# Layer 3's queries: stored as whole fp32 words by one eviction each, split into high and low part on GpSimd at load

## The reference, cut to what matters

```python
B, Q, S1, S2 = (4, 64, 512, 512)
D, H, K, F = (512, 16, 128, 2048)
def _cross_attention(q_in, kv_in, wq, bq, wk, bk, wv, bv, wo, bo, bias_k, bias_v):
    qh = (q_in @ wq + bq).reshape(b, q_len, H, K)
    kh = (kv_in @ wk + bk).reshape(b, t, H, K)
    vh = (kv_in @ wv + bv).reshape(b, t, H, K)
    kh = jnp.concatenate([kh, jnp.broadcast_to(bias_k, (b, 1, H, K))], axis=1)
    vh = jnp.concatenate([vh, jnp.broadcast_to(bias_v, (b, 1, H, K))], axis=1)
    logits = jnp.einsum('bqhk,bthk->bhqt', qh, kh) / scale
    weights = jax.nn.softmax(logits, axis=-1)
    ctx = jnp.einsum('bhqt,bthk->bqhk', weights, vh).reshape(b, q_len, H * K)
    return ctx @ wo + bo
```

## Time and profile before

| what | value |
|---|---|
| time, median of 3 runs | 2662.59 us |
| lowest and highest run | 2662.57 and 2664.82 us |
| span of the profiled execution | 2669.9 us |
| own run time of the profiled execution | not given |
| PE (matmul) busy | 2463.5 us, 92% |
| PEld (weight load) busy | 2167.2 us, 81% |
| DVE busy | 1386.4 us, 52% |
| ACT busy | 1151.4 us, 43% |
| POOL busy | 752.3 us, 28% |
| mean granted TensorE clock | 0.954 |
| DMA | 459.14 MB, mean 172 GB/s |

### The profile page before, as it was taken

The page is one execution under the profiler, slowest core; times in us unless marked ns, Lnnn a source line. Parts: engine busy times, 40 slices in busy tenths (PEclk is TensorE's granted clock), DMA queues, the critical chain, the costliest instruction groups (busy, mean ns, idle before and its releaser), DMA issues. The chain is left out here.

```text
span 2669.9 us, 37770 instructions
## 1 busy us (share of the span) xinstructions
PE 2463.5 (92%) x13976; PEld 2167.2 (81%) x13976; DVE 1386.4 (52%) x2360; ACT 1151.4 (43%) x2473; POOL 752.3 (28%) x386
## 2 busy tenths in 40 slices
PE   7898689989999699899899999979998999999698
PEld 5676334479896467799899999979998999999698
DVE  4666631268886633233366565633335656664632
ACT  3777112123332432223476666622236666664320
POOL 1100322262210450341153342406204343432300
PEclk9999879989999799899999999999999999999799
DMA  7553163489995146344876666525287666663300
GB/s 232 128 134 70 69 226 112 110 245 231 246 235 177 67 176 230 130 151 155 285 242 216 211 201 188 190 82 192 105 289 259 196 195 215 220 203 110 118 12 25
DMA packets 237306, 459.14 MB, mean 172 GB/s; under 512 B 90588, under 2 KB 133620, under 8 KB 236356
## 3 DMA queue, kind: packets, MB, share of 16 engines
q1 hardware_dynamic: 237124, 456.73, 55.1%
HBM read 345.46 MB, written 119.37 MB: 174 GB/s over the span
## 5 line engine op out<-in xcount | busy, mean ns | idle before, releaser
L2007 PE MATMUL att_ring<-ca_pp,att_arena 128*128 128x400 f32 (+1 forms) x2304 | 429.1, 344 | 9.6 <-issue 7.1
L2007 PEld LDWEIGHTS att_ring<-ca_pp,att_arena 128*128 128x128 f32 (+1 forms) x2304 | 415.4, 188 | 15.9 <-issue 15.9
L2077 POOL TENSOR_TENSOR att_arena<-att_arena 128x1448 fp32r<-128x1448 f32 x64 | 212.4, 3319 | 611.1 <-ACT att_arena L2084 611.1
L2007 PE MATMUL att_ring<-att_arena,qk_wh 128*128 128x362 f32 x1024 | 256.3, 332 | 0.0
L2699 DVE TENSOR_TENSOR ca_yl<-att_ring,att_arena 128x400 fp32r<-128x400 f32 x256 | 146.5, 572 | 188.4 <-ACT att_arena L2657 188.4
L2007 PE MATMUL att_ring<-att_arena,qk_wl 128*128 128x362 f32 x512 | 173.2, 338 | 18.4 <-POOL att_arena L2264 17.2
L2007 PEld LDWEIGHTS att_ring<-att_arena,qk_wh 128*128 128x128 f32 x1024 | 185.6, 192 | 0.0
L2657 ACT ACTIVATE att_arena<-att_ring 128x400 fp32r<-128x400 f32 x256 | 129.0, 504 | 82.7 <-PE att_ring L2007 82.7
L2090 ACT ACTIVATE att_kstage<-att_score,att_shift 100x362 f32<-100x362 f32 x256 | 143.9, 563 | 45.4 <-DVE att_shift L2103 45.3
L1075 ACT ACTIVATE rec_stage<-rec_fbank,rec_columns 128x361 f32<-128x361 f32 x128 | 72.2, 564 | 199.0 <-PE rec_fbank L2007 198.3
L2007 PE MATMUL att_score<-att_arena 128*100 128x362 f32 x768 | 145.2, 339 | 0.0
(11 more groups left out here) (408 smaller groups left out, 5895.1 us busy)
## 6 DMA issues: line engine op xcount, KB each, us to landing
att_arena<-ctx_parts SPq DMA_DIRECT2D x64, 1024.0 KB, 5.8
att_arena<-keys SPq DMA_DIRECT2D x64, 724.0 KB, 5.4
att_arena<-ctx_parts SPq DMA_DIRECT2D x64, 420.0 KB, 7.1
queries<-att_arena SPq DMA_DIRECT2D x64, 400.0 KB, 6.0
att_arena<-queries SPq DMA_DIRECT2D x64, 400.0 KB, 4.1
keys<-rec_stage SPq DMA_DIRECT2D x32, 724.0 KB, 4.3
keys<-att_kstage SPq DMA_DIRECT2D x32, 724.0 KB, 3.2
l_arena<-kept_value SPq DMA_DIRECT2D x176, 100.0 KB, 5.3
```

The lines of the kernel that those rows point to most:

```text
L2007: issued = nc.tensor.matmul(out, x, y, start=(first and k == 0), stop=(last and k == count - 1))
L2077: self.nc.gpsimd.tensor_tensor(self.kl[:, n % 2].bitcast(F32R), self.kl[:, n % 2], self.kh[:, n % 2].bitcast(F32), ALU.subtract).then_inc( ...
```

## The change

The query is evicted once, as whole fp32 words: heads 0 and 2 by ScalarE, heads 1 and 3 by VectorE (a tensor_scalar add of the bias), each engine waiting for the bank and the slot itself, and TensorE waits for that one eviction (`query_act` or `query_dve`). `qstage` now lies in `loose` and has the same two slots. A store and a load carry 200 KB. At a load, the whole words come to the place of the low part, and GpSimd makes the high part (add of zero, 128x400) and then the low part in place (subtraction, 128x400): `split_query`, issued behind each `low_key`. TensorE's scores wait for it (`q_ready`) and no longer for the load. At the start of `attention` the wait for all query stores goes from ScalarE to VectorE, whose output sums lie in `loose`.

```diff
...
 F3 = 2048
 RING = 4
+QS = 2
 W3 = G3 * K3
 BH = B // 2
...
         self.ring = [sc.bank(f"ring{i}") for i in range(RING)]
         self.score = [sc.bank(f"score{i}") for i in range(G3)]
-        self.queries_out = [[sc.sem(f"queries_out{k}{h}") for h in range(G3)] for k in range(2)]
+        self.queries_out = [[sc.sem(f"queries_out{k}{h}") for h in range(G3)] for k in range(QS)]
         self.q_in, self.k_in, self.x_in = ([sc.sem(f"{n}{i}") for i in range(2)] for n in ("q_in", "k_in", "x_in"))
...
             sp.wait_ge(self.score_full, G3 * (n - 1))
         g, b = n // B, n % B
-        sp.dma_start(self.q[:, n % 2].bitcast(F32), self.queries[g, :, :, :, b * L:(b + 1) * L]).then_inc(self.q_in[n % 2], 16)
+        sp.dma_start(self.q[:, n % 2, 1].bitcast(F32), self.queries[g, :, :, b * L:(b + 1) * L]).then_inc(self.q_in[n % 2], 16)
+
+    def split_query(self, pool, n):
+        whole = self.q[:, n % 2, 1].rearrange("p h l -> p (h l)")
+        high = self.q[:, n % 2, 0].rearrange("p h l -> p (h l)")
+        pool.wait_ge(self.q_in[n % 2], 16 * (n // 2 + 1))
+        if n >= 2:
+            pool.wait_ge(self.score_full, G3 * (n - 1))
+        self.nc.gpsimd.tensor_tensor(high, whole.bitcast(F32), self.nothing[:].broadcast_to([P, G3 * L]), ALU.add).then_inc(self.q_high, 1)
+        pool.wait_ge(self.q_high, n + 1)
+        self.nc.gpsimd.tensor_tensor(whole, whole.bitcast(F32), high.bitcast(F32), ALU.subtract).then_inc(self.q_ready, 1)
     def load_context(self, sp, n):
         if n >= 2:
...
         self.nc.vector.reciprocal(self.share[:, n % 2], self.total[:, n % 2]).then_inc(self.share_done, 1)
     def scores(self, pe, n):
-        pe.wait_ge(self.q_in[n % 2], 16 * (n // 2 + 1))
+        pe.wait_ge(self.q_ready, n + 1)
         pe.wait_ge(self.k_ready, n + 1)
         for h in range(G3):
...
     KSTEPS = NK * B
     KUNITS = KSTEPS * G3
-    QS, KS = 2, 2
+    KS = 2
     LN0 = 6
     CD = CC // 2
...
-        qstage = t.rest.rearrange("p (s i h n) -> p s i h n", s=QS, i=2, h=G3)
+        qstage = t.loose[:].rearrange("p (s h n) -> p s h n", s=QS, h=G3)
...
                     load_weights(NK + g + 2)
                 for h in range(G3):
-                    sp.wait_ge(query_low, G3 * k + h + 1)
-                    sp.dma_start(t.queries[g, :, :, h, half * HALF:(half + 1) * HALF], qstage[:, k % QS, :, h].bitcast(F32)).then_inc(
+                    sp.wait_ge((query_act, query_dve)[h % 2], 2 * k + h // 2 + 1)
+                    sp.dma_start(t.queries[g, :, h, half * HALF:(half + 1) * HALF], qstage[:, k % QS, h]).then_inc(
                         t.queries_out[k % QS][h], 16)
                 if k == 0:
...
                 pool.wait_ge(xn_ready, b + 1)
                 nc.gpsimd.tensor_tensor(X[:, b, :], X[:, b, :], bias[:], ALU.add).then_inc(bias_added, 1)
-            t.low_key(pool, 0)
-            t.low_key(pool, 1)
-            t.low_key(pool, 2)
+            for n in range(3):
+                t.low_key(pool, n)
+                t.split_query(pool, n)
         @block.scalar
         def _(act):
...
                 g, half = k // 2, k % 2
                 for h in range(G3):
-                    if k >= QS:
-                        act.wait_ge(t.queries_out[k % QS][h], 16 * (k // QS))
-                    act.wait_ge(full, KUNITS + G3 * k + h + 1)
-                    nc.scalar.activation(qstage[:, k % QS, 0, h, :], t.ring[h][:, 0:HALF], ACT.Identity,
-                                         bias=t.column[:, g * G3 + h, 0:1]).then_inc(query_high, 1)
+                    if h % 2 == 0:
+                        if k >= QS:
+                            act.wait_ge(t.queries_out[k % QS][h], 16 * (k // QS))
+                        act.wait_ge(full, KUNITS + G3 * k + h + 1)
+                    if h % 2 == 0:
+                        nc.scalar.activation(qstage[:, k % QS, h, :], t.ring[h][:, 0:HALF], ACT.Identity,
+                                             bias=t.column[:, g * G3 + h, 0:1]).then_inc(query_act, 1)
                     if half == 0 and NK + g + 1 < JOBS:
                         round_piece(NK + g + 1, h)
...
                     nc.vector.tensor_tensor(vdl[:], vd[:], vdh[:].bitcast(F32), ALU.subtract).then_inc(diff_low, 1)
                 for h in range(G3):
-                    dve.wait_ge(query_high, G3 * k + h + 1)
-                    nc.vector.scalar_tensor_tensor(qstage[:, k % QS, 1, h, :], t.ring[h][:, 0:HALF], t.column[:, g * G3 + h, 0:1],
-                                                   qstage[:, k % QS, 0, h, :].bitcast(F32), ALU.add, ALU.subtract).then_inc(query_low, 1)
+                    if h % 2 == 1:
+                        if k >= QS:
+                            dve.wait_ge(t.queries_out[k % QS][h], 16 * (k // QS))
+                        dve.wait_ge(full, KUNITS + G3 * k + h + 1)
+                        nc.vector.tensor_scalar(qstage[:, k % QS, h, :], t.ring[h][:, 0:HALF], t.column[:, g * G3 + h, 0:1], None,
+                                                ALU.add).then_inc(query_dve, 1)
                     if half == 0 and NK + g + 1 < JOBS:
                         low_piece(NK + g + 1, h)
...
                     pe.wait_ge((kept_act, kept_dve)[u % 2], u // 2 + 1)
                 else:
-                    pe.wait_ge(query_low, u - KUNITS + 1)
+                    v = u - KUNITS
+                    pe.wait_ge((query_act, query_dve)[v % 2], v // 2 + 1)
             def weight(j, h, c):
                 part = slice(h * K3, (h + 1) * K3)
...
             sp.wait_ge(cleared, 2)
             sp.wait_ge(t.parts_out, 32)
-            for s in range(2):
+            for s in range(QS):
                 for h in range(G3):
-                    sp.wait_ge(t.queries_out[s][h], 16 * NG3)
+                    sp.wait_ge(t.queries_out[s][h], 16 * (2 * NG3 // QS))
             for n in range(STEPS):
                 if n + 3 < STEPS:
...
                 if n + 3 < STEPS:
                     t.low_key(pool, n + 3)
+                    t.split_query(pool, n + 3)
                 g = n // B
                 if n % B == 1:
...
                 nc.scalar.activation(oh[:, h, :], bank_of("o", j, h)[:, 0:HALF], ACT.Identity,
                                      bias=column[:, j // 2 * G3 + h, 2:3]).then_inc(o_high, 1)
-            for s in range(2):
-                for h in range(G3):
-                    act.wait_ge(t.queries_out[s][h], 16 * NG3)
             for n in range(STEPS + 1):
                 if n < STEPS:
...
                 dve.wait_ge(rows_full, b + 1)
                 nc.vector.tensor_tensor(X[:, b, :], X[:, b, :], bank_of("rows", half, i)[0:L, :], ALU.add).then_inc(rows_added, 1)
+            for s in range(QS):
+                for h in range(G3):
+                    dve.wait_ge(t.queries_out[s][h], 16 * (2 * NG3 // QS))
             for n in range(STEPS + 3):
                 if n == STEPS:
...
 def attention_block(nc, a, X, spare, ident, column, i):
     weights = [a[f"L3_xattn_w{w}{i}"] for w in "qkvo"]
-    queries = nc.dram_tensor(f"queries{i}", (NG3, P, 2, G3, B * L), F32).ap()
+    queries = nc.dram_tensor(f"queries{i}", (NG3, P, G3, B * L), F32).ap()
     rows = nc.dram_tensor(f"rows{i}", (B, L, C), F32).ap()
     scratch = nc.dram_tensor(f"value_parts{i}", (2, H3, K3), F32).ap()
```

10 lines of the change are left out of this document (5 added, 5 removed).

## The result

| | before | after |
|---|---|---|
| median of 6 runs each, us | 2662.58 | 2649.23 |
| lowest and highest, us | 2658.16 and 2664.82 | 2646.57 and 2654.82 |
| profiled execution: span, us | 2669.9 | 2648.6 |

What follows compares the result with a forecast made beforehand. TensorE's waits in two stretches of layer 3 were taken as the bound. Gains of 8.8 + 3.9 + 2.8 + 0.8 - 4.0 = 12.3 us, off the median 2662.6, gave 2650.3 us, range 2644 to 2660.

Steps and rivals of the forecast that it cites:

- Query stage and its clock: Query stage, both blocks: TensorE's waits for query evictions go, 8.8 us, and the slow clock behind them, 3.9 us.
- The byte argument: Query stage: 11 transfers, each 200 KB smaller, 2.2 MB at 374 GB/s, let the deciding store land 5.9 us earlier.
- half the gap: Rival, 0.14: in the query stage only half the gap goes, since other transfers stay; gain 6.0 us, 2656.6.
- the gap moves: Rival, 0.10: query-stage banks would wait for weights loaded just before or VectorE's own slot; 2663.0, no change.
- if ScalarE or VectorE still stands over 8 us at a staging slot: Sign, in the profile after, by which the prediction would call itself wrong.
- End of the projections: Barrier before attention: VectorE takes the last query, ScalarE's exponentials start earlier; 1.4 us per block, 2.8 us.
- Second attention step: Bank waits behind ScalarE's keys: the query load ahead is 0.2 MB smaller; 0.4 us per block, 0.8 us.
- The pair on GpSimd: The query's two split operations, taken as 1.9 us; hidden in steady attention steps within 3.97 us, cost 0.
- The first steps: First attention steps: scores 0.8 us late, output weights and the keys behind them 1.2; -4.0 us over two blocks.
- the first steps pay nothing: Rival, 0.08: in the first attention steps keys land earlier by as much as GpSimd is later; 2646.3.
- The port: VectorE's shift waits out the GpSimd operation it meets, then slips in before the next; the pair costs nothing more.
- the port is not given back: Rival, 0.06: VectorE's shift waits for the query pair too; 14 steps stop TensorE up to 1.9 us each, 2676.9.

Runs made afterwards that it cites:

- e1: The kernel before with three staging slots for the queries in place of two, stores still 400 KB; 2655.86 us, ratio 0.9972.
- e2: The changed kernel with each query stored twice, so stores are 400 KB again and loads stay at 200 KB; 2659.21 us, ratio 0.9982.
- e7: The changed kernel with VectorE's shift made by an operation with one SBUF input in place of two; 2652.56 us, ratio 0.9958.
- e12: The changed kernel with GpSimd splitting only head 0's columns, all four heads' scores made from them; 2650.11 us, ratio 0.9949.
- e3: The changed kernel with ScalarE and VectorE swapped, ScalarE evicting heads 1 and 3 and so the last query; 2658.82 us, one run.
- e6: The changed kernel with step 3's key and query loads and step 1's context load issued early, in the projections; 2650.22 us, ratio 0.9951.
- e8: The changed kernel with e6's early loads and the query's split put ahead of the key's low part on GpSimd; 2641.99 us, ratio 0.9924.
- e4: The changed kernel with the high part of every query made five times over on GpSimd, a pair of 5.7 us; 2694.2 us, one run.
- e9: The changed kernel with the shift made by ScalarE and no longer by VectorE; 2652.22 us, ratio 0.9958.
- e10: The changed kernel with e6's early loads and the shift made by ScalarE; 2649.11 us, ratio 0.9948, four runs.

## Why the prediction was right, point by point

**Query stage and its clock: right, a little low.** Predicted 8.8 + 3.9 = 12.7 us, measured 13.5 (the table's first column). The byte argument gave a landing 5.9 us earlier, the trace 5.0 to 5.5 in the first block and at least 6.6 in the second. Of the margin of 6.5 against 4.7, 1.8 us, the trace leaves 1.1. e1 shows the slot as the cause, e2 the bytes. The rival "half the gap" fell by this margin, which e7 and e12 show to be thin; "the gap moves" fell with the trace of after, in which PE waits at no bank of this stage (e1 shows 1.3 us of it). The path is not quite the text's. Its eleven transfers do not stand in one queue: the four stores of half 0 have landed (27.05 us in) before SP issues the two loads (27.45). What comes earlier is above all the issue of the deciding store, at 31.87 in place of 36.25 us in, 4.4 of the 5.5 us; its own landing took 12.6 in place of 13.7. And one of the prediction's own signs of being wrong appeared: "if ScalarE or VectorE still stands over 8 us at a staging slot". ScalarE stood for 10.56 us, and this cost nothing, since what counts is when the eviction ends and not how long ScalarE has stood.

The 5.0 us that the prediction worked out from the Trainium skill (DMA: Bandwidth & Descriptors, Anatomy of one DMA: a fixed part that does not shrink with the size, beside bytes at a higher rate) is an estimate, and that section measures DMAs that GpSimd issues, where these are issued by SP. With 5.0 to 5.5 us in one block and at least 6.6 in the other, no run here decides between it and the 5.9 of the byte rate.

For the other terms further marks are needed, in the same unit as the table's: the first transposes after the barrier (step 0), those of step 1, and the scores of step 5.

| kernel | transposes 0 | transposes 1 | scores 5 |
|---|---|---|---|
| before | 84.50, 84.57 | 96.47, 97.90 | 119.57, 121.30 |
| after | 76.14, 76.14 | 87.50, 88.94 | 111.66, 112.91 |
| e1 | 79.36, 78.06 | 91.48, 90.25 | 113.42, 112.30 |
| e3 | 77.85, 77.78 | 89.16, 90.41 | 114.01, 114.36 |

**End of the projections: right, a little low.** Predicted PEq 3.2 to about 1.8 and 2.8 us. Measured 1.5, and from the scores of step 1 to the transposes of step 0 1.64 us less in each block, 3.3 in all (the 3.8 above has 0.5 us of a slower clock behind the barrier in it). The ends of ScalarE and VectorE and the start of TensorE, each on its timeline in after:

```profile
1312.59 0.22 ACT L2101 ACTIVATION_READ_ACCUMULATOR att_kstage<-att_score,att_shift 100x1 f32 x1
```

```profile
1312.26 0.63 DVE L2444 TENSOR_SCALAR att_loose<-att_ring,att_columns 128x400 f32<-128x400 f32 x1 [3.77 <-PE att_ring L2008]
```

```profile
1313.68 1.22 PE L2771 MATMUL att_ring<-state_ident,att_kstage 100*128 100x100 f32 x12 [1.54 <-PEq L35]
```

Both end within 0.1 us of each other, VectorE last at 1312.89, as the text had it. Then SP issues the last store, on the timeline of SP in after:

```profile
1312.92 0.32 SPq L2255 DMA_DIRECT2D queries<-att_loose  x1
```

It ends at 1313.24, and TensorE goes on 0.44 us later, near the 0.4 that the text took. What the text did not count is that this issue is shorter for the smaller store (0.32 us, 0.51 before). e3 shows that the swap of the last head is what the rest hangs on. VectorE's new wait (2.12 us, at L2709) stayed behind its cover, as said.

**Second attention step: right, 0.8 predicted and 1.1 measured.** TensorE's waits for the banks did not shrink (1.6 and 3.6 us before, 1.9 and 3.7 now), but they are a poor measure, since TensorE arrives earlier too. The transposes of step 1 start 4.5 us after the landing of step 3's keys in both blocks of before and of after, and the keys landed 4.94 and 6.31 us after their issue before, 4.36 and 5.82 now: 0.6 and 0.5 us less, for a query load of 200 KB less ahead of them. From the transposes of step 0 to those of step 1 it is 0.61 and 0.53 us less. ScalarE still waited 4.99 us at its high key, first in before, then in after:

```profile
1333.77 1.41 ACT L2084 ACTIVATE att_arena<-att_arena 128x1448 fp32r<-128x1448 f32 x1 [4.99 <-DMA att_arena<-keys]
```

```profile
1320.53 1.41 ACT L2095 ACTIVATE att_arena<-att_arena 128x1448 fp32r<-128x1448 f32 x1 [4.99 <-DMA att_arena<-keys]
```

e6 and e8 show what decides there: a load that is issued only after the barrier. With that load moved ahead, no bank wait at the transposes of step 1 is left.

**The pair on GpSimd: right.** Taken at 1.9 us; L2071 and L2073 have medians of 0.854 and 1.049, together 1.90. In the steady steps it is hidden, and the slack of 3.97 us was confirmed by e4 (1.5 us too late with a pair that is 1.7 too long).

**The first steps: this term failed.** The text had -4.0 us: "two pairs stand in this chain, 3.8 us: 0.8 too late (taken as alike in both blocks)", and "I take 1.2" for the output weights and the keys behind them. From the transposes of step 1 to the heads the traces differ by 0.25 and 0.07 us, -0.3 in all. The 0.8 is there: from the transposes of step 1 to the scores of step 5 the change takes 1.06 and 0.57 us more, 1.6 in all (in the first block a slower clock behind the bank wait is in it, not separated), and GpSimd ends the pair just ahead of these scores (1348.93 and 1349.19 in the first block). The 1.2 was found nowhere, and this is the step that failed: ScalarE's wait for those keys went from 1.12 to 1.66 us in one block and from 2.75 to 1.25 in the other, the scores that need them (step 6) follow their transposes within 1.0 us in both blocks, and from the heads to the next scores TensorE takes 16.9 us before and after. So the lateness of loads and helper engines was handed to TensorE without asking whether TensorE was waiting there.

And 1.3 us came back that the text did not have: from the scores of step 5 to the heads the change takes 0.81 and 0.50 us less. Before, TensorE waited there for a bank, on its timeline in before:

```profile
1372.12 0.55 PE L2753 MATMUL att_ring<-state_ident,att_kstage 100*106 100x100 f32 x4 [0.33 <-DVE ca_yl L2699]
```

With the change there is no such wait. VectorE's shift ahead of it took 2.77 and 2.49 us before and 0.35 and 1.57 now, since it meets GpSimd at another place. That this is the cause was not tested.

The small total is thus a matter of what else holds TensorE, and not a price of the split as such. In e1, which has no split and a barrier wait of 3.2 us, the stretch from the transposes of step 1 to the heads is 35.0 and 34.4 us; in e3, which has the split and the same barrier wait, it is 37.4 and 37.2. That is 5.2 us more, 3.6 of them waits for the split at L2073, though e1 and e3 differ in more than the split. The waits at L2073 over both blocks are 0.8 us in after, 1.6 in e7, 2.7 in e2, 2.8 in e9, 3.2 in e10 and 3.6 in e3. The rival "the first steps pay nothing" (0.08) was nearer in the number, by another reason than it gave.

**The port.** "It waits out the operation it meets and slips in before the next" holds in most cases, not in all. I held every shift of after against GpSimd's timeline. Of 64, ten met a free GpSimd, 52 ended with the instruction that they met, and two met the key split and ended 0.8 us after it, with the first half of the query split. In the traces of e2, e6 and e12 there are four more that went past the instruction they met (one, two and one), and all six ended with the first half of a query split. One of the two, on the timelines of DVE and POOL in after:

```profile
1679.84 3.07 DVE L2114 SCALAR_TENSOR_TENSOR att_shift<-att_top,att_zeros 100x4 f32<-100x4 f32 x1
```

```profile
1678.75 3.33 POOL L2088 TENSOR_TENSOR att_arena<-att_arena 128x1448 fp32r<-128x1448 f32 x1
1682.03 0.87 POOL L2071 TENSOR_TENSOR att_arena<-att_arena,att_nothing 128x400 fp32r<-128x400 f32 x1
1682.97 1.05 POOL L2073 TENSOR_TENSOR att_arena<-att_arena 128x400 fp32r<-128x400 f32 x1
```

It ends at 1682.91. So "the port is not given back" happens, in 2 steps of 64 here and not in 14 at 1.9 us each. The chance of 0.06 was for its price, and e9 shows no price that can be measured in the changed kernel; e6 shows the same mechanism costing time where the instructions in the queue are long and the step is tight.

**The sum.** 12.3 predicted; by the marks 13.5 + 3.3 + 1.1 - 0.3 = 17.6, by the medians 13.4. Three terms were too small by 0.8, 0.5 and 0.3 us, and a term of the first steps was 3.7 too costly. By the marks the sum is 5.3 us too low. That it is off by only 1.1 against the medians is in part luck. Of the 21.3 us between the two traces, 17.6 are in these stretches, 4.3 ahead of layer 3's first query stage; 1.3 are lost between the blocks and 0.8 gained behind the second. Why the marks give 4 us more than the medians is open.

## What to carry to other kernels

Where an eviction waits for its staging slot, count the bytes ahead of the deciding store in the queue, and then the margin; and look whether a further slot does the same without a new format (here it gave 11.6 of the query stage's 13.5 us). Work moved to an engine that runs in order costs what it delays, not what it lasts: put first what is ready first, since a wait of that engine for another engine's result is free room, and the same 1.9 us that were harmless in e8 stood in the way in e6. And when one early wait is taken away, look two or three steps on before the edit is called useless: the best kernel here (2641.99 us, 0.9924 of before) is two edits of which neither alone gained anything that the medians could tell.

## What was not expected of the hardware

A 100x4 operation on VectorE that takes 0.16 us alone can take 6.47 us. While GpSimd worked through three instructions without a pause (the end of a 4.68 us one, 3.30 and 0.87), VectorE got its turn only in the pause of 0.08 us before the fourth. In most cases (52 of 54 in after) it does get in between two GpSimd instructions that follow each other at once; what decides is open. The number of SBUF inputs made no difference here: the one-input form has the same median, 2.08 us, and all 54 of its shifts that met a GpSimd instruction ended with it. The Trainium skill (SBUF — State Buffer, Who interferes with whom) names two ways for a VectorE instruction to need the shared port, two SBUF inputs or a fast mode that takes both port pairs, and counts the tensor_scalar form among those that can have such a mode; my form for e7 went from the first way to what may be the second. The same section of the Trainium skill also states that ScalarE never waits for this port. The trace agrees: the same work on ScalarE took 0.19 to 0.23 us in all 64 cases, with GpSimd as busy as before.
